# A graph-attention layer on one core: the first row group's adjacency in unit parts, x between the parts, and a new order of GpSimd's work

## The reference

```
h   = max(layernorm(x), 0)
Wh  = h @ W;   f1 = Wh @ a[:128];   f2 = Wh @ a[128:]
e   = leaky_relu(f1[:, None] + f2[None, :], 0.2)
e   = where(adj == 0, -inf, e)
out = x + softmax(e, axis=1) @ Wh
```

## Time and profile before

| | us |
|---|---|
| median of 3 runs (836.43 to 836.5) | 836.5 |
| the profiled execution's own time | 836.72 |
| its span | 835.1 |
| PE busy | 790.1 (95%) |
| DVE busy | 758.2 (91%) |
| ACT busy | 487.9 (58%) |
| POOL busy | 411.2 (49%) |

### The profile page before, as it was taken

One profiled execution on the slowest core, in us unless ns is written; L12 is line 12 of the kernel. 1 busy time (PEld: TensorE's weight loads), 2 busy tenths in 40 slices (PEclk: granted clock), 3 DMA queues, 4 the chain that ended last, 5 costly groups with the idle time before them and its releaser, 6 DMA issues.

```text
span 835.1 us, 22635 instructions
## 1 busy us (share of the span) xinstructions
PE 790.1 (95%) x8969; PEld 722.9 (87%) x8969; DVE 758.2 (91%) x1243; ACT 487.9 (58%) x793; POOL 411.2 (49%) x606
## 2 busy tenths in 40 slices
PE   3578989999999999999999999999999999999995
PEld 2467879999999999999999999999999999999995
DVE  4699999999999999999999999999999999999995
ACT  4477975555565555555565555555565556555541
POOL 4655656554554446554554446554554446553410
PEclk9899999999999999999999999999999999999998
DMA  9997579999999999999999999999999999997200
GB/s 222 116 108 69 51 73 105 105 87 98 98 90 101 88 107 87 101 87 98 96 90 101 87 106 89 101 87 102 95 88 101 87 109 84 103 86 80 27 15 16
DMA packets 43281, 75.99 MB, mean 91 GB/s; under 512 B 4720, under 2 KB 6896, under 8 KB 43248
## 3 DMA queue, kind: packets, MB, share of 16 engines
q0 software_dynamic: 38400, 67.13, 87.2%
q1 hardware_dynamic: 4432, 8.39, 2.9%
q10 hardware_dynamic: 416, 0.07, 0.0%
HBM read 272.70 MB, written 4.19 MB: 332 GB/s over the span
## 4 chain that ended last, share of the span: by engine, by line
PE 85%; DVE 7%; DMA 4%; ACT 2%; issue 1%; POOL 1%; ACTq 0%; DVEq 0%; POOLq 0%
PE acc L376 51%; PE acc L380 26%; PE stage L365 6%; DMA masks<-in_adj_dram 4%; DVE wt_ring L784 4%; DVE pairs L774 1%; DVE packed L766 1%; PE stage L356 1%; DVE stats L719 1%; ACT masks L559 0%; DVE packed L765 0%; PE stage L348 0%; ACT marks L541 0%; ACT wh L519 0%; ACT pairs L596 0%
## 5 line engine op out<-in xcount | busy, mean ns | idle before, releaser
L784 DVE SCALAR_TENSOR_TENSOR wt_ring<-stage,packed,marks 128x512 f32<-128x512 f32 x1024 | 697.7, 744 | 47.9 <-PE acc L380 41.9
L376 PE MATMUL acc<-pairs,wt_ring 128*128 128x258 f16 x4096 | 721.2, 274 | 9.1 <-DVE pairs L774 8.7
L380 PE MATMUL acc<-pairs,wt_ring 128*128 128x129 f16 x4096 | 699.6, 219 | 0.0
L376 PEld LDWEIGHTS acc<-pairs,wt_ring 128*128 128x128 f16 x4096 | 396.9, 97 | 65.1 <-issue 8.6
L541 ACT ACTIVATE marks<-stage 128x1024 uint16<-128x1024 uint8 x256 | 261.9, 1023 | 292.5 <-PE stage L365 291.5
L380 PEld LDWEIGHTS acc<-pairs,wt_ring 128*128 128x128 f16 x4096 | 400.4, 98 | 2.5
L193 POOL DMA_DIRECT2D masks<-in_adj_dram x252 | 137.7, 549 | 329.7 <-PE stage L365 306.7
L215 POOL TENSOR_TENSOR masks<-masks 128x256 int32<-128x256 int32 x256 | 179.5, 738 | 14.5 <-ACT masks L559 13.6
L559 ACT ACTIVATE masks<-masks 128x512 uint16<-128x512 uint16 x252 | 156.4, 622 | 8.3 <-DMA masks<-in_adj_dram 8.3
L365 PE MATMUL stage<-ident,masks 128*128 128x128 f32 x512 | 99.5, 276 | 2.6 <-ACT fin L632 2.0
L365 PEld LDWEIGHTS stage<-ident,masks 128*128 128x128 f32 x512 | 54.2, 142 | 6.3 <-ACT fin L632 2.3
(11 more groups left out here) (62 smaller groups left out, 161.1 us busy)
## 6 DMA issues: line engine op xcount, KB each, us to landing
masks<-in_adj_dram POOLq DMA_DIRECT2D x256, 256.0 KB, 7.1
out_dram<-xm SPq DMA_DIRECT2D x16, 256.0 KB, 7.5
xm<-in_x_dram SPq DMA_DIRECT2D x3, 1024.0 KB, 15.5
xm<-in_x_dram SPq DMA_DIRECT2D x1, 768.0 KB, 6.2
xm<-in_x_dram SPq DMA_DIRECT2D x1, 256.0 KB, 3.1
wx<-in_L_gnn_W_dram ACTq DMA_DIRECT2D x1, 64.0 KB, 3.3
a_sb<-in_L_gnn_a_dram ACTq DMA_DIRECT2D x1, 1.0 KB, 6.2
```

Of the source, the lines that this page charges most:

```text
L376: return nc.tensor.matmul(acc[:, r, 0:2 * E1], wtv[:, w, r, 1, :], pairv[:, t, :, 0:E1], start=st, stop=end)
L380: return nc.tensor.matmul(acc[:, r, 0:E1], wtv[:, w, r, 0, :], pairv[:, t, 0, 0:E1], start=False, stop=False)
L784: nc.vector.scalar_tensor_tensor(out=wtq[:, t % NW], in0=e_row, scalar=packed[:, t, 1:2], in1=edges[:, k], op0=ALU.max, op1=ALU.mult).then ...
```

## The change

- Row group 0's adjacency is loaded as 16 parts, one for each unit (load_part, first_loaded has 16 semaphores); load_rows goes. EARLY = 10 parts are issued before anything else on GpSimd, two after mix(1), four more after b = 0 and b = 1.
- SyncE's loads of x are 1, 3, 2, 4 and 6 groups; the last three wait for parts 0, 1 and 4.
- ScalarE's second starts with unit 2 and runs at b+3 (table SECONDS), in the steady loop 6 units ahead (AHEAD = 6). GpSimd does only units 0 and 1.
- GpSimd's turn b begins with a wait for low_part(b+1) (pair_ready), then mix(b+2) (before: mix(b+4), no such wait), normalise(b+4) (three of four slices, before two), scaled(b+2), which waits for pack(b+2) rather than for exponentials(b+2), and then loads. load_first and load_second of the next row group's chunk are both issued at b = 2, 6, 10 and 14.
- ScalarE's turn is unpack(b+1), high_part(b+1), second, keep(b+2, 0), root, keep(b+2, 1), exponentials(b+2), relu(b+3), normalise(b+4) (one slice, before two). scaled(0) goes from ScalarE to GpSimd; the Square of the weights goes to the start.
- VectorE's weights of a unit are made as two blocks, low_part, two blocks. Statistics come two groups at a time (table STATS), moments and inverses at b = 0, 2 and 6 (table LAST).
- TensorE's products of row group 0 run with the weight block k outside and the output block r inside, and wait for each block by itself; features(b+2, 0) after k = 0, x_transposes(b+3) after k = 1, transposes(b+2) and features(b+2, 1) after k = 2. In the prologue W's transpose and a's product go to the stage banks and features(0, 1) to acc[0].

```diff
-    AHEAD = 8
+    AHEAD = 6
+    EARLY = 10
-    BATCHES = [(0, 1), (1, 4), (4, 8), (8, 12), (12, 16)]
+    BATCHES = [(0, 1), (1, 4), (4, 6), (6, 10), (10, 16)]
+    STATS = {0: (4, 5), 1: (6, 7), 2: (8, 9), 4: (10, 11), 5: (12, 13), 6: (14, 15)}
+    LAST = {0: 2, 2: 3, 6: 4}
+    SECONDS = {0: (2,), 1: (3,), 2: (4, 5), 13: (16,), 14: (17, 18), 15: (19, 20, 21)}
+    MIXES = {13: (15, 16), 14: (17, 18), 15: (19,)}
...                                          SyncE
-            for k in range(len(BATCHES)):
+            load_x(0)
+            load_x(1)
+            for k, part in ((2, 0), (3, 1), (4, 4)):
+                sp.wait_ge(first_loaded[part], 16)
                 load_x(k)
...                                          GpSimd
+            def load_part(u):
+                c, k = u // KC, u % KC
+                nc.gpsimd.dma_start(masks[:, c * PACK:(c + 1) * PACK, k * BANK:(k + 1) * BANK],
+                                    adj_first[0, u]).then_inc(first_loaded[u], 16)
...
+            second(0)
+            mix(0)
+            second(1)
+            scaled(0)
+            mix(1)
+            load_part(EARLY)
+            load_part(EARLY + 1)
+            scaled(1)
             for b in range(UN):
+                if b + 1 < NQ:
+                    pool.wait_ge(s["pair_ready"], b + 2)
+                for u in MIXES.get(b, (b + 2,)):
+                    mix(u)
+                if b + 4 < NQ:
+                    normalise(b + 4)
+                if b + 2 < NQ:
+                    scaled(b + 2)
+                for u in range(EARLY + 2 + 2 * b, min(EARLY + 4 + 2 * b, UN)):
+                    load_part(u)
                 if b % KC == 2:
                     load_first(NC + b // KC)
-                if 1 <= b < NQ - 1:
-                    scaled(b + 1)
-                if b + 4 < NQ:
-                    normalise(b + 4)
-                mix(b + KC)
-                if b % KC == KC - 1:
-                    load_second(NC + 1 + b // KC)
+                    load_second(NC + b // KC)
+            load_second(2 * NC)
...                                          TensorE, turn b of row group 0 (b < 15)
+                for k in range(PACK):
+                    pe.wait_ge(s["weighted"], b * PACK + k + 1)
+                    for r in range(PACK):
+                        product(b, r, k)
+                    if b + 2 < NQ and k == 0:
                         features(b + 2, 0)
+                    if b + 3 < NQ and k == 1:
+                        x_transposes(b + 3)
...
+                    if k == 2:
                         pe.wait_ge(s["marked"], b + 2)
                         transposes((b + 2) % UN, b + 2)
+                        if b + 2 < NQ:
+                            features(b + 2, 1)
...                                          ScalarE, turn b
                 if b + 1 < UN:
                     unpack(b + 1, b + 1, first=True)
                 if b + 1 < NQ:
                     high_part(b + 1)
+                for u in SECONDS.get(b, (b + 3,)):
+                    second(u // UN, u % UN)
                 if b + 2 < NQ:
                     keep(b + 2, 0)
+                if b in LAST:
+                    root(LAST[b])
                 if b + 2 < NQ:
                     keep(b + 2, 1)
                     exponentials(b + 2)
+                if b + 3 < NQ:
+                    relu(b + 3)
+                if b + 4 < NQ:
+                    normalise(b + 4)
...                                          VectorE
-                weights(1, b)
+                weights(1, b, range(0, HALF))
+                low_part(b)
+                weights(1, b, range(HALF, PACK))
...
+                for g in STATS.get(b, ()):
+                    statistics(g)
+                if b in LAST:
+                    moments(LAST[b])
                 if b + 1 < NQ:
                     first_weights(b + 1)
-                    low_part(b + 1)
+                if b in LAST:
+                    inverses(LAST[b])
```

More of the change, by code:

```diff
@@ L137, in gat_kernel @@
         adj_second = [s[f"adj_second{c}"] for c in range(NC)]
-        first_loaded = [s[f"first_loaded{k}"] for k in range(KC)]
+        first_loaded = [s[f"first_loaded{k}"] for k in range(UN)]
         x_loaded = [s[f"x_loaded{k}"] for k in range(len(BATCHES))]
@@ L229, in normalise @@
                 pool.wait_ge(s["xt_ready"], g - 1)
-                for r in range(HALF, PACK):
+                for r in range(1, PACK):
                     t = g * PACK + r
@@ L367, in transposes, with product, high, lower @@
                 mm.then_inc(s["transposed"], 1)
[L369 to L389, removed]
+            def product(b, r, k):
+                w, t = (b * PACK + k) % NW, b * PACK + k
+                st, end = b == 0 and k == 0, b == UN - 1 and k == PACK - 1
+                def high():
+                    return nc.tensor.matmul(acc[:, r, 0:2 * E1], wtv[:, w, r, 1, :], pairv[:, t, :, 0:E1],
+                                            start=st, stop=end)
+                def lower():
+                    return nc.tensor.matmul(acc[:, r, 0:E1], wtv[:, w, r, 0, :], pairv[:, t, 0, 0:E1],
+                                            start=False, stop=False)
+                if end:
+                    lower()
+                    mm = high()
+                else:
+                    high()
+                    mm = lower()
+                if end and r < PACK - 1:
                     mm.then_inc(s["acc_done"], 1)
-                if r == PACK - 1:
+                if k == PACK - 1 and r == PACK - 1:
                     mm.then_inc(s["used"], 1)
@@ L501, in normalise @@
                     act.wait_ge(s["xt_ready"], g - 1)
-                for r in range(HALF):
+                for r in range(HALF if g < 4 else 1):
                     t = g * PACK + r
@@ L513, in relu, with keep @@
                 nc.scalar.activation(ht[:, g % 2, :], stage[:, 2, :], ACT.Relu).then_inc(s["ht_ready"], 1)
-            def keep(g, h):
+            def keep(g, h, bank=None):
+                fresh = stage[:, 3, :] if bank is None else acc[:, bank, :]
                 act.wait_ge(s["whp_ready"], 2 * g + h + 1)
@@ L555, in second @@
                 c, k = b // KC, b % KC
[L556 to L557 removed]
+                if isinstance(q, int) and q == 0:
+                    act.wait_ge(first_loaded[b], 16)
+                elif k == 0:
+                    act.wait_ge(adj_second[c], q * 2 * 16)
                 sl = slice(k * BANK // 2, (k + 1) * BANK // 2)
@@ L616, in _ @@
             relu(0)
+            keep(0, 0)
             root(1)
-            normalise(1)
-            keep(0, 0)
+            keep(0, 1, bank=0)
+            exponentials(0)
+            unpack(0, 0, first=True)
+            high_part(0)
             relu(1)
[L621 to L625, removed]
             keep(1, 0)
-            normalise(2)
-            relu(2)
             keep(1, 1)
             exponentials(1)
+            relu(2)
             normalise(3)
-            nc.scalar.activation(squares, acc[:, 0, 0:P], ACT.Square,
-                                 accum_out=lim[:, 2:3]).then_inc(s["norms_ready"], 1)
             for b in range(UN):
@@ L636, in _ @@
                     unpack(b + 1, b + 1, first=True)
-                if b + 3 < NQ:
-                    relu(b + 3)
-                for u in (range(2 * b - 6, 2 * b - 4) if b >= 10 else range(b + KC, b + KC + 1)):
-                    if u < UN + AHEAD:
-                        second(u // UN, u % UN)
                 if b + 1 < NQ:
                     high_part(b + 1)
+                for u in SECONDS.get(b, (b + 3,)):
+                    second(u // UN, u % UN)
                 if b + 2 < NQ:
                     keep(b + 2, 0)
-                if b == 0:
-                    root(2)
-                if b + 4 < NQ:
-                    normalise(b + 4)
+                if b in LAST:
+                    root(LAST[b])
                 if b + 2 < NQ:
@@ L753, in normalise @@
                     dve.wait_ge(s["xt_ready"], g - 1)
-                for r in range(HALF, PACK):
+                for r in range(HALF if g in (0, 3) else 0, PACK):
                     t = g * PACK + r
@@ L776, in low_part, with weights @@
                                                op1=ALU.add).then_inc(s["pair_ready"], 1)
-            def weights(bank, b):
+            def weights(bank, b, blocks=range(PACK)):
                 edges = marks[:, b % MR, :].rearrange("p (s w h) -> p s h w", s=PACK, h=2)
                 e_row = stage[:, bank, :].rearrange("p (h k) -> p h k", h=2)
-                for k in range(PACK):
+                for k in blocks:
                     t = b * PACK + k
```

127 lines of the change are left out of this document (51 added, 76 removed).

## The result

| | before | after |
|---|---|---|
| median, us | 836.46 (834.31 to 836.5, 4 runs) | 842.27 (841.99 to 842.44, 4 runs) |
| span of the profiled execution, us | 835.1 | 840.7 |
| VectorE busy, us | 758.2 | 744.9 |

The changed kernel is slower: the ratio is 1.0085, 95% interval 1.0071 to 1.0098. The forecast was 842.5 us. The spans differ by 5.6 us and the medians by 5.8; the kernel before varies from run to run, between 834 and 836.5, which is why the ratio says a little more.

The account below looks back on a forecast made before the run. A hand-over chain of 6.66 us a unit, no full engine, was taken to bound row group 0: 835.1 + 5.3 + 0.7 for the clock = 841.1 span, 842.7 execution, median 842.5 us; range 838 to 847, wider 831 to 849.

Parts of the forecast that it names:

- What bounds: Whole kernel: TensorE fills row group 1, so only the start of unit 15's products counts, 118.3 us before, 123.6 forecast.
- The start: Row group 0's beginning: adjacency parts land earlier, unit 1's weights start at 25.2 us, 5.8 earlier; low_part(1) ends at 27.2.
- The ring: Row group 0: hand-over chain from low_part(b+1) through mix, transposes, features, ScalarE and weights to low_part(b+2), 6.66 us a unit.
- The moments: VectorE at b = 2 and 6: pack, two statistics and moments delay the weights, 1.0 us twice.
- three shares of 0.3 for load issues: GpSimd at b = 2, 6 and 10: four load issues end near the next low_part, about 0.3 us each.
- 0.7 for the clock: TensorE in row group 0: a few spells at the 1.2 GHz level after idle gaps add 0.7 us.
- VectorE's lock: VectorE operations held up by GpSimd's: 8.8 us excess, returned in full by the skill's rule, worth nothing by the prediction.
- The busiest engine's pace (812): Rival, row group 0: hand-overs overlap, TensorE's 4.6 us a unit sets the pace, about 812 us; chance 0.10 with milder form.
- The short ring: Rival, row group 0: hand-over chain only 6.1 to 6.2 us, median 835 or 832; chance 0.22 for under 6.4.
- the clock in most units: Rival: TensorE drops to 1.2 GHz after its gap in most units, 0.6 us more 14 times, 850 us; chance 0.10.
- Parts no earlier: Rival, the beginning: adjacency parts land no earlier than 14.2 us, everything 3 to 4 us later, 846; chance 0.08.
- The milder form: Rival: VectorE is the path, its 8.8 us and the start's 5.8 come back, 822; within the first rival's chance 0.10.

Follow-up runs that it names:

- e5: The changed kernel with all five loads of x issued at once, without waiting for adjacency parts: 848.15 us, 1.0144 of the kernel before.
- e7: The changed kernel with ScalarE's second and GpSimd's mix one unit further ahead in row group 0, GpSimd's wait for low_part(b+1) kept: 823.69 us.
- e3: The changed kernel with GpSimd's scaled(g) waiting for the exponentials alone, not for pack(g): 846.32 us, 1.0120 of the kernel before.
- e9: e7 with GpSimd's scaled(g) waiting for the exponentials alone, not for pack(g): 826.61 us, 0.9893 of the kernel before.

## Why the prediction was right, point by point

- **What bounds.** Right: no engine's busy time, but the time to unit 15's first product. Behind it nothing moved, except 0.5 us at the border (that product 5.1 later, the span's end 5.6), where unit 16's products waited 0.72 for their weights. I had nothing for that.
- **The start.** low_part(1) ended at 26.8; forecast 27.2. The way there differs. Part 0 was there by 9.5 and part 1 by 12.0, not at 10.5 and 14.3; what came next was VectorE's normalise(1), 2.43 us for four slices beside GpSimd's work, and TensorE's x_transposes(1) at 15.4. The two errors cancel, and that is luck. That x's place behind the parts is worth 5.5 us is shown by e5; no run has the small parts changed by themselves.
- **The ring.** Forecast 6.66, measured 6.63 in seven of the 14 rounds, and the last two 6.25 and 5.77 for 6.27 and 5.79. Link by link two errors cancel: GpSimd's end to TensorE's start, for which no row was at hand, took 0.15 and not 0.07, and transposes with features took 0.85 and not 0.92. The moments cost 0.9 us in each of their two rounds (7.52 and 7.56), forecast 1.0. The three shares of 0.3 for load issues weren't there: a mix behind four issues started at once (48.74). In their place three rounds took 7.31, 7.00 and 7.32: in each of these TensorE was at the 1.2 GHz level for a time (granted 0.50 in 28:29, 44:46 and 72:73). In these keep(b+2, 1) starts 1.71, 1.40 and 1.71 us behind the mix's end and not 1.04, so the time is lost in TensorE's link. They add up to 1.7 us, where I had 0.9 for loads and, outside the rounds, 0.7 for the clock. So two small terms were wrong and nearly made up for each other. Sum of 14 rounds: 95.2 measured, 95 forecast. e7 shows that the ring was the cause: the same work with the mix one unit earlier is 18.6 us faster.
- **VectorE's lock.** Here the prediction was wrong in what it stated. It said that the time VectorE gets back is worth nothing since VectorE doesn't set the pace. e3 and e9 show 3 to 4 us for the hold-off of scaled: pack stands ahead of the statistics, and in those turns these end when unpack does (60.01 and 59.82 above), so that any more of VectorE's time is on the ring. The prediction had this only for the two turns with moments. Its sum wasn't hit, because it counted with undisturbed packs. That the one that comes second waits for the whole of the other's instruction is what the Trainium skill says (SBUF — State Buffer, "Who interferes with whom"). The trace agrees: L783 starts at 61.56 and ends at 62.48, GpSimd's multiply runs from 61.40 to 62.45.
- **The rivals.** The busiest engine's pace (812) fell. The short ring and the clock in most units didn't come; the clock did in three, for 1.7 us where I had added 0.7 (0.4 to 0.7 a round, for the rival's 0.6). Parts no earlier: refuted. The milder form, 822 with VectorE as the path, fell too, though its condition came true: L786 and L794 are back at 171 and 689 ns, and the kernel is slower.
- **AHEAD = 6** and the loads of the next row group: nothing, as forecast; row group 1's TensorE is full.

## What to carry to other kernels

A wait that keeps one engine's work off another's is free only as long as what it holds back isn't due next: count the units of lead between the gated operation and its reader, and follow the chain from the gate through each in-order engine back to the gate. If it closes within one unit, its length can be the pace, however idle the engines are: here one more unit of lead gave 18.6 us, taking the gate away 10.2, and the one shortening that was tried 4.3. And an order that is right under one limit has to be tried again under the next one: the same edit gave 4.3 us and cost 4.3 us.

## What the runs showed that I had not expected

- The pace of this ring could be worked out from durations in the other kernel's trace to 0.03 us in 6.6; single links were off by up to 0.08.
- VectorE's four normalise slices took 2.43 us beside GpSimd's multiplies in the changed kernel's start, and the four of the next group 1.12 a moment later (12.89 and 15.74). The trace tells which of GpSimd's instructions stood beside them: the third slice starts at 13.58 and takes 1.06, beside scaled(0) from 13.48 to 14.56, and the fourth starts at 14.56 and takes 0.77, beside mix(1) from 14.52 to 15.24. In e5, where GpSimd stands idle at that time, the same four slices take 1.11.
- VectorE's slack in the statistics turns was next to nothing, so 0.75 us more in pack showed in the time although VectorE is busy only 40.1 of 65 us over 54:119.
